# Block norms as one rounded product, and the last block in three pieces

## The reference, cut to what matters

```
xn = layernorm(x)
y  = xn @ U                        # 128 -> 32
n  = sum(y*y, -1)
attn = softmax(-(n_i + n_j - 2 y_i.y_j))
out  = x + attn @ xn + ffn(xn)     # shared FFN (1024) + 8 experts (512), top 2,
                                   # capacity 320 tokens, router on RMS-normed xn
```

## Time and profile before

| | |
|---|---|
| median of runs | 164.44 us |
| the profiled execution, its own time | 163.57 us |
| its span | 161.8 us |
| granted TensorE clock, mean | 1.0 |
| PE busy | 157.2 us (97%) |
| DVE busy | 122.8 us (76%) |
| ACT busy | 102.9 us (64%) |
| POOL busy | 77.0 us (48%) |

### The profile page before, as it was taken

One profiled execution on the slowest core, in us unless ns is written; L12 is line 12 of the kernel. 1 busy time (PEld: TensorE's weight loads), 2 busy tenths in 40 slices (PEclk: granted clock), 3 DMA queues, 4 the chain that ended last, 5 costly groups with the idle time before them and its releaser, 6 DMA issues.

```text
span 161.8 us, 3141 instructions
## 1 busy us (share of the span) xinstructions
PE 157.2 (97%) x983; PEld 137.6 (85%) x983; DVE 122.8 (76%) x302; ACT 102.9 (64%) x216; POOL 77.0 (48%) x87
## 2 busy tenths in 40 slices
PE   5999999999999999999999999999999999999993
PEld 6977675696789998888888899999999999978992
DVE  4899969897964369999998857877867867645962
ACT  3359686339979819786875566998876675534200
POOL 7061120057777777887100000579888884456000
DMA  5999999941111110743656400052241310017586
GB/s 139 275 277 126 234 310 319 345 147 49 56 50 62 53 39 15 195 135 93 203 173 184 138 0 2 0 162 71 88 106 45 84 34 24 28 41 216 140 272 195
DMA packets 26335, 20.73 MB, mean 128 GB/s; under 512 B 2285, under 2 KB 22280, under 8 KB 26320
## 3 DMA queue, kind: packets, MB, share of 16 engines
q1 hardware_dynamic: 24528, 17.89, 41.5%
q0 software_dynamic: 1792, 2.65, 5.2%
HBM read 12.36 MB, written 7.92 MB: 125 GB/s over the span
## 4 chain that ended last, share of the span: by engine, by line
PE 87%; DVE 8%; DMA 2%; issue 1%; ACT 0%
PE bank L1108 14%; PE bank L1110 14%; PE bank L1109 14%; PE bank L1250 9%; PE bank L1188 9%; PE bank L1298 5%; PE bank L1296 5%; PE bank L1297 5%; PE bank L1173 2%; PE bank L1161 2%; PE bank L1312 2%; DVE stats L773 2%; DVE row L803 2%; DMA acc<-in_L_attn_x_dram 2%; PE bank L1323 2%; DVE mv L780 1%
## 5 line engine op out<-in xcount | busy, mean ns | idle before, releaser
L597 ACT ACTIVATE silu<-bank 128x512 f32<-128x512 f32 (+1 forms) x64 | 33.2, 520 | 31.2 <-PE bank L1110 31.0
L504 POOL DMA_INDIRECT slots_dram<-row,slot_i x32 | 34.0, 1061 | 22.3 <-issue 22.3
L932 DVE TENSOR_TENSOR bank<-bank,silu 128x320 f32<-128x320 f32 (+1 forms) x48 | 27.1, 565 | 15.2 <-ACT silu L597 12.6
L523 POOL DMA_INDIRECT routed_dram<-eo,xg x24 | 23.0, 957 | 11.6 <-DVE eo L972 6.4
L938 DVE TENSOR_TENSOR hid_lo<-bank,hid_hi 128x320 fp32r<-128x320 f32 (+1 forms) x48 | 26.2, 547 | 0.0
L1108 PE MATMUL bank<-xnT_hi,sw_hi 128*128 128x512 f32 x62 | 25.0, 404 | 0.0
L1110 PE MATMUL bank<-xnT_hi,sw_lo 128*128 128x512 f32 x62 | 24.3, 392 | 0.0
L1109 PE MATMUL bank<-xnT_lo,sw_hi 128*128 128x512 f32 x62 | 24.2, 390 | 0.0
L605 ACT CAST hid_hi<-bank 128x320 fp32r<-128x320 f32 (+1 forms) x48 | 23.0, 478 | 0.0
L511 POOL TENSOR_TENSOR ew_lo<-sw_raw,ew_hi 128x1024 fp32r<-128x1024 f32 x3 | 7.3, 2419 | 24.6 <-ACT ew_hi L621 24.6
L1188 PEld LDWEIGHTS bank<-row,probs 128*128 128x128 f32 x128 | 14.8, 191 | 1.1 <-ACT probs L589 0.9
(11 more groups left out here) (181 smaller groups left out, 322.4 us busy)
## 6 DMA issues: line engine op xcount, KB each, us to landing
sw_raw<-in_L_ffn_rg_dram SPq DMA_DIRECT2D x8, 256.0 KB, 2.8
sw_raw<-in_L_ffn_ru_dram SPq DMA_DIRECT2D x8, 256.0 KB, 3.2
rd_raw<-in_L_ffn_rd_dram SPq DMA_DIRECT2D x8, 256.0 KB, 3.2
routed_dram<-fill SPq DMA_DIRECT2D x1, 2048.0 KB, 12.5
routed<-routed_dram SPq DMA_DIRECT2D x8, 256.0 KB, 4.0
slots_dram<-fill SPq DMA_DIRECT2D x1, 1300.0 KB, 12.6
xg<-slots_dram SPq DMA_DIRECT2D x8, 130.0 KB, 2.4
acc<-in_L_attn_x_dram SPq DMA_DIRECT2D x4, 256.0 KB, 3.8
```

What stands on the lines that cost most here:

```text
L504: G.indirect_dma_start(slots_dram, bass.IndirectOffsetOnAxis(slot_i[:, k, t:t + 1], 0), row[:, t, 0:RW], None, bounds_check=E * CAP - 1, o ...
L523: G.indirect_dma_start(routed_dram, bass.IndirectOffsetOnAxis(xg[0:n, e % XB, r, 1:2].bitcast(I32), 0), eo[0:n, e % 2, r, :], None, bounds ...
L597: C.activation(silu[:, q % 2, 0:n], gate_bank(q)[:, 0:n], ACT.Silu).then_inc(silu_ready, 1)
L932: V.tensor_tensor(hid, up[:, 0:n], silu[:, q % 2, 0:n], ALU.mult).then_inc(hid_ready, 1)
```

## The change

The norms become one fp32r product. ysq is computed on 64 partitions (two of the three copies of y). ACT rounds it to `ysq_parts` (`ysq_hi`). In the second 32 partitions the remainder is put in place of the rounded square, by POOL for blocks 0 and 1 and by DVE (`ysq_lo`) for 2 and 3. PE then multiplies 64 rows by a half of 64x128, so that the norm fills all 128 rows of the bank; it waits for the remainder and for y_lo of that block (`y_lo_s`), since y is overwritten.

Block 2's y moves to bank 5 and block 3's to bank 6 (`y_b`). The queues change their order: on PE, projection 2 and norms 0 and 1 lie between the down tiles, projection 3 ahead of scores 0, and attend(b, 0) ahead of scores(b + 1); on ACT, y_hi(2) and ysq_hi(2) stand ahead of n_hi(0), and exps(2) and exps(3) ahead of n_left(3) and of the rounding of expert 0's weights; on DVE, y_lo(1) stands ahead of n_lo(0), and ysq_lo(2) and ysq_lo(3) are added. lgT is kept in turned_out. The last block ends in three pieces of 2, 1 and 1 tiles, each with its own sum and its own DMA.

```
-        half = sb("half", [R, 4])
+        half = sb("half", [2 * R, P], F32R)
+        END_PIECES = [(bank[6], 0, 2), (bank[5], 2, 1), (bank[7], 3, 1)]
+        y_b = [bank[6], bank[7], bank[5], bank[6]]
@@ POOL, after split_shared(3)
+            for g in range(2):
+                pool.wait_ge(ysq_hi_s, g + 1)
+                G.tensor_tensor(ysq_parts[R:2 * R, g, :], ysq[R:2 * R, g, :],
+                                ysq_parts[R:2 * R, g, :].bitcast(F32), ALU.subtract).then_inc(ysq_split_pool, 1)
+                pool.wait_ge(ysq_split_pool, g + 1)
@@ ACT, y_hi(g): the wait on n_done for g >= 2 stays
-                C.activation(ysq[:, g % 2, :], turn_b[g % 2][0:R, :], ACT.Square).then_inc(ysq_ready, 1)
+                C.activation(ysq[:, g % 2, :], y_b[g][0:2 * R, :], ACT.Square).then_inc(ysq_ready, 1)
+            def ysq_hi(g):
+                act.wait_ge(ysq_ready, g + 1)
+                C.copy(ysq_parts[:, g % 2, :], ysq[:, g % 2, :]).then_inc(ysq_hi_s, 1)
@@ ACT, order
-            n_hi(0)
             silu_chunk(6)
             silu_chunk(7)
+            ysq_hi(0)
+            ysq_hi(1)
             act.wait_ge(e2_asked, 1)
             C.activation(e2[:, :], m2[:, :], ACT.Exp).then_inc(e2_ready, 1)
+            y_hi(2)
+            ysq_hi(2)
+            n_hi(0)
             n_left(0)
             n_hi(1)
-            y_hi(2)
             exps(0)
             n_left(1)
             n_hi(2)
             y_hi(3)
+            ysq_hi(3)
             exps(1)
             n_left(2)
             n_hi(3)
+            exps(2)
             n_left(3)
-            exps(2)
+            exps(3)
             round_weights(0, 0)
             round_weights(0, 1)
             act.wait_ge(sd_loaded, 16)
-            exps(3)
@@ DVE
+            def ysq_lo(g):
+                dve.wait_ge(ysq_hi_s, g + 1)
+                V.tensor_tensor(ysq_parts[R:2 * R, g % 2, :], ysq[R:2 * R, g % 2, :],
+                                ysq_parts[R:2 * R, g % 2, :].bitcast(F32), ALU.subtract).then_inc(ysq_split_dve, 1)
@@ DVE, order
             y_lo(0)
+            y_lo(1)
             n_lo(0)
-            y_lo(1)
+            ysq_lo(2)
             n_lo(1)
+            y_lo(2)
             block_sum(0)
             dve.wait_ge(block_added, 1)
-            y_lo(2)
             n_lo(2)
+            ysq_lo(3)
             y_lo(3)
@@ PE, norms and projection
+                elif g == 2:
+                    pe.wait_ge(pos_ready, 1)
                 else:
-                    pe.wait_ge(y_ready, g - 1)
+                    pe.wait_ge(y_ready, 1)
-                pe.wait_ge(ysq_ready, g + 1)
-                M(turn_b[g % 2][NR, :], half[:, :], ysq[:, g % 2, :], start=True, stop=True
+                if g < 2:
+                    pe.wait_ge(ysq_split_pool, g + 1)
+                else:
+                    pe.wait_ge(ysq_split_dve, g - 1)
+                pe.wait_ge(y_lo_s, g + 1)
+                M(y_b[g][:, :], half[:, :], ysq_parts[:, g % 2, :], start=True, stop=True
@@ PE, order
-            norms(0)
             for c in range(6, CS):
                 up_of_block(0, c)
             ranks()
+            down_first_block([0])
+            project(2)
+            down_first_block([1])
+            norms(0)
+            down_first_block([2])
             norms(1)
-            down_first_block(range(0, TG - 1))
-            project(2)
+            project(3)
             scores(0)
-            down_first_block(range(TG - 1, TG))
+            down_first_block([TG - 1])
             norms(2)
-            project(3)
             for b in range(B):
+                attend(b, 0)
                 if b + 1 < B:
                     scores(b + 1)
-                attend(b, 0)
+                attend(b, 1)
                 if b == 0:
                     norms(3)
-                attend(b, 1)
@@ PE, down_end_block (xg_ready, out_copied and eo_ready are waited for first)
+                for o, i, _ in END_PIECES:
+                    down_tile(o[:, 0:D], i, range(CS - 2))
                 pe.wait_ge(hid_ready, at["block", b, CS - 1] + 1)
+                for o, i, n in END_PIECES:
+                    last = down_tile(o[:, 0:D], i, range(CS - 2, CS))
+                    for j in range(1, n):
+                        last = down_tile(o[:, D * j:D * j + D], i + j)
+                    last.then_inc(end_down, 1)
```

More of the change, by code:

```diff
@@ L226, in moe_attention_kernel @@
         turned_out = sb("turned_out", [P, S])
+        lgT = turned_out
         eo = sb("eo", [P, 2, 3, D])
@@ L231, in moe_attention_kernel @@
             probs = room.enter_context(nc.sbuf_tensor("probs", [P, 2, TG, S], F32))
-            ysq = room.enter_context(nc.sbuf_tensor("ysq", [R, 2, S], F32))
+            ysq = room.enter_context(nc.sbuf_tensor("ysq", [2 * R, 2, S], F32))
+            ysq_parts = room.enter_context(nc.sbuf_tensor("ysq_parts", [2 * R, 2, S], F32R))
             norm_parts = room.enter_context(nc.sbuf_tensor("norm_parts", [P, S], F32R))
-            lgT = room.enter_context(nc.sbuf_tensor("lgT", [P, S], F32))
         with ExitStack() as room:
@@ L301, in moe_attention_kernel @@
         ysq_ready, n_done, nhi_ready = sem("ysq_ready"), sem("n_done"), sem("nhi_ready")
+        ysq_hi_s, ysq_split_pool, ysq_split_dve = sem("ysq_hi_s"), sem("ysq_split_pool"), sem("ysq_split_dve")
+        y_lo_s = sem("y_lo_s")
         norm_split, yL_ready = sem("norm_split"), sem("yL_ready")
@@ L432, in _ @@
                 sp.dma_start(out_v[g], acc[:, TG * g:TG * g + TG, :]).then_inc(out_written, 16)
-            for h in range(2):
+            for h, (_, i, n) in enumerate(END_PIECES):
                 sp.wait_ge(block_added, B + h)
-                sp.dma_start(out_v[B - 1][:, 2 * h:2 * h + 2, :],
-                             acc[:, TG * (B - 1) + 2 * h:TG * (B - 1) + 2 * h + 2, :]).then_inc(out_written, 16)
-            sp.wait_ge(out_written, 16 * (B + 1))
+                t = TG * (B - 1) + i
+                sp.dma_start(out_v[B - 1][:, i:i + n, :], acc[:, t:t + n, :]).then_inc(out_written, 16)
+            sp.wait_ge(out_written, 16 * (B - 1 + len(END_PIECES)))
         @block.gpsimd
@@ L754, in _ @@
             V.memset(fill[:, 2:RW], 0.0).then_inc(fill_zeroed, 1)
-            V.memset(half[:, :], -0.5)
+            V.memset(half[:, :].bitcast(F32), -0.5)
             V.memset(rwT[:, :, :].bitcast(F32), 0.0).then_inc(rwT_zeroed, 1)
@@ L896, in y_lo @@
                 cols = slice(S * g, S * g + S)
-                ps = turn_b[g % 2]
+                ps = y_b[g]
                 dve.wait_ge(y_hi_s, g + 1)
@@ L977, in end_block_sum @@
                 dve.wait_ge(end_down, h + 1)
-                t = TG * (B - 1) + 2 * h
-                a = acc[:, t:t + 2, :].rearrange("p t d -> p (t d)")
-                V.tensor_tensor(a, (turn_b[0], sums_b)[h][:, 0:2 * D], a, ALU.add).then_inc(block_added, 1)
+                o, i, n = END_PIECES[h]
+                t = TG * (B - 1) + i
+                a = acc[:, t:t + n, :].rearrange("p t d -> p (t d)")
+                V.tensor_tensor(a, o[:, 0:n * D], a, ALU.add).then_inc(block_added, 1)
             def add_routed(k, g):
@@ L1097, in _ @@
             dve.wait_ge(summed, 2 * B)
-            end_block_sum(0)
-            end_block_sum(1)
+            for h in range(len(END_PIECES)):
+                end_block_sum(h)
         @block.tensor
@@ L1184, in attend @@
                 else:
-                    pe.wait_ge(pos_ready, 1)
+                    pe.wait_ge(y_ready, 3)
                 for i in range(2 * h, 2 * h + 2):
```

22 lines of the change are left out of this document (8 added, 14 removed).

## The result

| | before | after |
|---|---|---|
| median of the timed runs | 164.39 us (4 runs) | 169.18 us (167.72 to 170.07, 4 runs) |
| ratio, 95% interval | | 1.0294 [1.0256, 1.0331] |
| profiled execution, its span | 163.57, 161.8 | 168.69, 167.2 |
| attention ends (first chunk of block 1) | 59.21 | 62.50 |
| block 1, first chunk to its turn | 22.72 | 23.13 |

The change costs 4.8 us, where 1.65 was forecast: the direction was right, the size was not, and 169.2 lies above the range of 164.9 to 167.4. A second timing of the same two kernels, on another occasion, gave 168.81 us against 164.19, 1.0270 [1.0224, 1.0315]. Of the 5.4 us between the two spans 3.29 fall before block 1 begins, 0.63 in blocks 1 and 3, 1.03 in one interval between experts, and 0.47 at the end. The last two are no cost of the change, as will be seen.

The account below looks back on a forecast made before the run. PE was taken as the bound (87% of the chain, full from 24.4 to 59.2 us). Profiled 163.57 + 1.75 (attention) - 0.1 (end) = 165.2; as median 164.44 + 1.65 = 166.1 us, range 164.9 to 167.4.

Parts of the forecast that it names:

- step 1: PE around chunk 7 and the ranks: waits of 0.68 and 0.36 us for DVE; down tile 0 starts at 29.27.
- Price of the norm: On PE: each new fp32r norm takes 0.33 us instead of 0.94, removing 2.44 over four; bounds 0.24 and 0.94.
- Step 2: Norm 0 on PE: DVE starts y_lo(0) at 32.6, so norm 0 waits 0.18 us and starts at 33.99.
- Rival B: POOL's subtractions beside DVE's routing contend for the SBUF interface: routing +0.5 us, each stretched n_lo +0.27; 167.1 us; chance 0.13.
- Where on POOL they cost nothing: POOL splits ysq 0 and 1, 1.30 us each, from 28.3 to 30.9, hidden; on DVE up to 1.4 later.
- Step 3: Before projection 3 and scores 0, PE waits 1.93 us for y_ready 1, since y_hi(2) and ysq_hi(2) precede n_hi(0) on ACT.
- Steps 4 to 6: PE from scores 0 to the attention's end: waits of 0.08, 0.42, 0.09 and 0.49 us, then full, ending at 60.86.
- the walk: PE, DVE and ACT queues followed side by side from 24.42: waits 4.23 us against 2.58 less work, attention 1.65 later.
- After 59 us everything follows PE: the delay stays.: From block 1 on: the attention's delay carries through unchanged; the wider memset of half costs nothing.
- The end, -0.1: Last block in three pieces: one more DMA issue, smaller last transfer; sum -0.1 us, bounds -0.3 and +0.45.
- Rival D: PE's granted clock falls after the 1.93 us wait; 4 us at half speed cost 2, giving 168.1; chance 0.03.
- Rival A: PE stays full in the attention, paying only two waits, 1.04 us in all; faster, 162.9 us; chance 0.07.

Follow-up runs that it names:

- pool_late: The changed kernel with GpSimd's second subtraction held back until DVE's routing is over; 199.95 against 196.81 us for before, ratio 1.0148, on a chip with the standstill.
- ring3: The changed kernel with three places for the squares, so y_hi(g) waits for norm g-3; 200.24 against 196.81 us for before, ratio 1.0182, with the standstill.
- reordered_b: The mended kernel with the PE, DVE and ACT queues ordered anew; 164.19 against 164.28 us for before, ratio 1.0001, without the standstill.
- mended kernel: After with late second subtraction, three square places, n_hi(0) before ysq_hi(2), two end pieces, half last, four idle products; 1.0144, 1.0112, 1.0022 to before, with the standstill.
- after_again: The changed kernel run again, unchanged, on another occasion; 168.81 against 164.19 us for before, ratio 1.0270.

## Why the prediction was right and wrong

- **What bounds the kernel, and the direction.** Right: PE was full, and taking norms from ahead of chunk 7 and the ranks gave waits of 0.58 and 0.28 where 0.68 and 0.36 were forecast (step 1).
- **Price of the norm.** 0.39 at norm 0 (34.96 to 35.35) against 0.33 in the sum; norms 2 and 3 took 0.47 and 0.46 (43.48 to 44.36 and 49.11 to 49.95, waits taken off). Mis-sized by 0.06 to 0.14 each.
- **Step 2, start of y_lo(0) at 32.6.** This is the step that failed on the path: the term for the two subtractions on POOL was put at nothing, and it cost 0.94. y_lo(0) came at 33.42, for the comparison that stood 0.94 for POOL, and norm 0 at 34.96 instead of 33.99. Rival B named the mechanism and gave it 0.5 for a whole microsecond of routing and 0.13 of chance. Its size came from one stretched row, as if the two engines shared a port in proportion; pool_late and the ends of the rows show that this instruction of DVE, with two SBUF inputs, does not get done until POOL's is, and so 0.29 became 1.23. The Trainium skill, SBUF — State Buffer, "SBUF: two separate sides", tells of an exclusive lock for the whole instruction, against a GpSimd operation that reads SBUF, with the later one blocked; the trace agrees (the comparison starts at 29.86, after POOL's second subtraction at 29.68, and ends at 31.09, after 30.94). By that section of the Trainium skill the wait could have been worked out beforehand as the rest of POOL's second subtraction, which the prediction had ending at about 30.9; I had only weighed the shorter statement of the Trainium skill, GPSIMD Engine Reference, "Specifications".
- **"Where on POOL they cost nothing".** Wrong for the same reason. The cover was looked for on PE and POOL (norm 0 needs the result at 34.0), not on DVE.
- **Step 3, the wait before projection 3.** Right in place, cause and size: 2.00 against 1.93, and 1.66 of it goes with ring3. It began 1.30 later (37.83 against 36.53), 0.97 of that from norm 0, and ended 1.37 later (39.83 against 38.46). On the way n_lo(0)'s second instruction took 0.76 (forecast 0.55, B: +0.27).
- **Steps 4 to 6.** Waits 0.41 and 0.38 (0.42 and 0.49), and none at norms 2 and 3 (0.08 and 0.09). From scores 0 to block 1 the walk has 21.62 and the trace 21.90. Against the walk, the trace is 0.97 late at norm 0, 1.36 at scores 0, 1.49 at attend(0,0), 1.67 at attend(1,0) and 1.64 at the end of the attention.
- **"After 59 us everything follows PE: the delay stays."** The second step that failed, by 0.63 in the stages: the wider `half` was priced as a memset and not as a change of every address behind it. No row of before could show this; that an allocation moves others was there to be seen in the diff.
- **The end, -0.1.** Right within what can be told (0.0 between the means of eight and eleven traces). The 0.2 taken off for a smaller transfer is borne out: over the eight traces with three pieces the 64 KB land in 1.95 in the mean (1.7 to 2.1, each the median of two), and over all traces the 128 KB in 2.4 (2.1 to 2.7).
- **Rival D, chance 0.03.** Its event comes in three of six traces and, by the mean clocks, in five of eight executions; the step that failed is "a wait of 1.93 should not lose it". One fall costs 1.56 in the trace (D: 2). I had taken (0.36 of work in 2 us, clock 1.00) as proof that 1.93 of standing is harmless; the same row after two waits in a row was not there to be read.
- **Rival A.** Refuted in this order, and not reached in the best order that was tried either: with waits of 0.51 left in all from norm 0 on, the attention ends at 59.46, no earlier than before.

The sum: 3.3 for the attention (1.65 forecast, 0.94 for the comparison, 0.7 smaller prices), 0.6 for the addresses, 0.6 for the clock as estimated above, 0 at the end: 4.5, against 4.6 and 4.8 measured. The first term is read from the trace; the second is read from the stages and not borne out in full by the times; the third is an estimate. Three causes, the comparison, the ring and the addresses, were each undone by themselves in a trace. That nothing else of size is left is shown by reordered_b, which is as fast as before, with the reservation that it also changes the order. The mended kernel alone was not timed on a chip without the standstill. What holds the engines there, and which part of the fall of the clock belongs to the first wait (1.13) and which to the second, stays open.

## What to carry to other kernels

Before work is given to an idle GpSimd, look at what VectorE does beside it: here an operation with two SBUF inputs, 0.29 long, stood until GpSimd's subtraction of 1.30 was over, so the price (0.94) was set by the rest of GpSimd's instruction and was no share of it. GpSimd's scatter did not do this: ysq_lo, with two SBUF inputs as well, took 0.68 to 0.75 beside it. A shorter operation on a full engine pays only if the next one is ready; here the first of the old, dear norms stood in a place that PE lost anyway once it was gone, and even the best order that was tried gained nothing. A tile that changes its size changes the address of all behind it: put it last, and look at stages that the change does not touch.

## What the runs showed of the hardware

- An fp32r product of 512 columns is issued every 0.229 to 0.230 us with its tiles at 0 mod 64 bytes and every 0.232 with them at 32, in the mean of blocks 1 and 2, at clock 1.00.
- POOL's subtraction over 32 partitions takes 1.30, as over 128.
- DVE's scan (L893, 0.41) and another operation that reads a bank (L894, 0.29) ran undisturbed beside POOL's subtraction; the comparison with both inputs in SBUF did not (1.23).
- The granted clock fell to the lower of its two levels (1.2 GHz) in some executions of a program and not in others, after the same waits (1.13 and 2.00; mean 0.81 in 36 to 45 us in after_again, 1.00 in after), and in one trace of the eight with waits of 0.6 and 0.3 behind these (0.51 in 29.4 to 32.8, pool_late).
- On three chips ACT and DVE stand up to 28 us at a time ("remote") while POOL scatters; on another chip the same programs (before and reordered) don't. The cause is open.
